# Three PSUM banks that rotate between the two products of a scan step, and one 128-row product for dt's factor, B and C

## The reference, cut to what matters

```python
xs = silu(conv3(x_c));  x_dbl = xs @ W_x.T           # W_x: (64 + 16 + 16) x 256
dt_param, Bp, Cp = x_dbl[..., :64], x_dbl[..., 64:80], x_dbl[..., 80:]
dt = softplus(dt_param @ W_dt.T + b_dt) + 1e-05
A_disc = exp(-exp(A_log) * dt[..., None])             # one factor for each of 16 states
Bx = Bp[:, :, None, :] * dt[..., None] * xs[..., None]
s = A_t * s + Bx_t;  ssum = s.sum(-1)                 # a scan over the tokens for each state
y = (Cp @ W_C.T) * ssum + D_param * xs
```

## Time and profile before

| | |
|---|---|
| three runs | 1262.65, 1260.84, 1262.3 us; median 1262.3 |
| profiled execution | 1258.12 us; its span 1256.3 us |
| busy share of the span | TensorE 83%, VectorE 56%, GpSimd 54%, ScalarE 50% |
| mean granted clock of TensorE | 0.901 of full |

### The profile page before, as it was taken

How to read it: one execution, slowest core, us unless ns; L and a number is a source line. 1 busy time by engine, 2 the same in 40 slices (tenths; PEclk the granted TensorE clock), 3 DMA queues, 4 the chain that set the end, 5 groups by cost and what they waited for, 6 DMA issues and landing times. The chain is left out here.

```text
span 1256.3 us, 15452 instructions
## 1 busy us (share of the span) xinstructions
PE 1043.6 (83%) x4736; PEld 832.8 (66%) x4736; DVE 705.6 (56%) x1280; ACT 625.3 (50%) x1190; POOL 681.0 (54%) x605
## 2 busy tenths in 40 slices
PE   4555578887867887797988899969999999999995
PEld 2122265664644655575777688859999999999884
DVE  1699998999988899976796442101111111111045
ACT  3784869778476586668554432212232222232234
POOL 2495967759469786578665347324343433332221
PEclk9676778898887897898999899979999999999998
DMA  5000010202002007113322589359998888887252
GB/s 180 18 28 6 34 34 18 68 1 83 2 1 84 1 18 227 42 22 110 83 96 67 172 236 208 55 150 347 337 316 266 264 276 251 262 273 227 41 176 101
DMA packets 140931, 162.68 MB, mean 129 GB/s; under 512 B 27976, under 2 KB 125984, under 8 KB 140832
## 3 DMA queue, kind: packets, MB, share of 16 engines
q1 hardware_dynamic: 124976, 142.70, 36.0%
q0 software_dynamic: 15872, 18.99, 7.7%
HBM read 135.20 MB, written 26.87 MB: 129 GB/s over the span
## 5 line engine op out<-in xcount | busy, mean ns | idle before, releaser
L1542 POOL TENSOR_TENSOR Ssum<-Ssum,S 128x512 f32<-128x512 f32 x240 | 301.5, 1270 | 105.9 <-DVE S L1162 104.7
L1014 PE MATMUL psum<-w,hT 128*128 128x256 f32 x1152 | 260.0, 384 | 4.2 <-issue 4.2
L1014 PEld LDWEIGHTS psum<-w,hT 128*128 128x128 f32 x1152 | 219.8, 193 | 34.4 <-issue 4.6
L1592 POOL DMA_INDIRECT acc_d<-y,ID x72 | 114.3, 1587 | 236.8 <-DMA acc_d<-y,ID 124.7
L1431 ACT ACTIVATE A<-dts,nea 128x512 f32<-128x512 f32 x256 | 177.3, 720 | 68.6 <-DVE S L1162 40.4
L1470 ACT ACTIVATE hT<-psum,bb 128x256 f32<-128x256 f32 x200 | 83.5, 470 | 244.7 <-PE psum L981 244.7
L981 PE MATMUL psum<-XT,w 128*128 128x256 f32 x800 | 182.8, 386 | 7.4 <-issue 6.5
L1138 DVE TENSOR_TENSOR psum<-us,psum 128x512 f32<-128x512 f32 x256 | 163.4, 682 | 31.6 <-PE psum L902 29.6
L981 PEld LDWEIGHTS psum<-XT,w 128*128 128x128 f32 x800 | 154.0, 194 | 33.9 <-issue 10.7
L1162 DVE TENSOR_TENSOR_SCAN S<-A,carry,psum 128x512 f32<-128x512 f32 x120 | 148.8, 1264 | 0.0
L1296 DVE TENSOR_TENSOR y<-bb,psum 128x256 f32<-128x256 f32 x72 | 27.0, 416 | 209.0 <-PE psum L1014 209.0
(11 more groups left out here) (149 smaller groups left out, 1314.3 us busy)
## 6 DMA issues: line engine op xcount, KB each, us to landing
w<-W SPq DMA_DIRECT2D x94, 1024.0 KB, 6.7
bb<-b SPq DMA_DIRECT2D x47, 128.0 KB, 7.8
xnb<-x SPq DMA_DIRECT2D x16, 256.0 KB, 3.0
Xr<-x SPq DMA_DIRECT2D x16, 256.0 KB, 4.6
x_d<-gb SPq DMA_DIRECT2D x8, 512.0 KB, 2.9
xn_d<-nb SPq DMA_DIRECT2D x8, 512.0 KB, 3.3
X<-x_d SPq DMA_DIRECT2D x16, 256.0 KB, 9.3
ACC<-acc_d SPq DMA_DIRECT2D x16, 256.0 KB, 5.9
```

What stands on the lines that cost most here:

```text
L1014: t = eng.matmul(bank(g)[:, 256 * k:256 * k + 256], hT[n % 2][:, f, 128 * k:128 * k + 128], w[:, f, :], start=f == 0, stop=f == 7)
L1542: eng.tensor_tensor(to, to, of, ALU.add).then_inc(nsum, 1)
L1592: eng.indirect_dma_start(acc_d, bass.IndirectOffsetOnAxis(ap=ID[:, col, 1:2].bitcast(u32), axis=0), y[n % NY][:, k, :], None, compute_op=A ...
```

## The change

1. The three banks rotate. `spread` of step m writes bank m mod 3. The first product of `mult` writes bank (m - 1) mod 3, which the step before has used, the second goes in place as before. `spread` then waits for one scan less, `mult` for one scan more.
2. `dtc` and `bp` become one product `dbc` of 128 rows: four times 16 rows of B (in the fourth, of C) and 16 rows of dt's factor. It is copied once to f32 (`dbc`) and once to bf16 (`bst`). `dt` then multiplies 128 rows, with zeros in `wdt` where B and C stand; `cmat` reads rows 96 to 111. `dbc_out` stands in PLAN where `bp_out` stood.
3. At the start the zeroing of `wx` on GpSimd and the wait for it go; `wx` is loaded by 8 DMAs in place of 5, and `wdt` is 128 x 256 in place of 64 x 256.
4. The five other banks rotate over one use less in each chunk, so that some products take a bank that another one has left.

```diff
-        BB, UB = PS[0:2], PS[2]
+        BB = PS[0:3]
...
-                        eng.wait_ge(scan, 2 * (m - 1))
-                    eng.matmul(BB[m % 2], SEL[:, n:n + 1].to_broadcast([96, 128]), bst[i % 2],
+                        eng.wait_ge(scan, 2 * m - 3)
+                    eng.matmul(BB[m % 3], SEL[:, n:n + 1].to_broadcast([96, 128]), bst[i % 2],
...
-                    bb = BB[m % 2]
+                    bb, ub = BB[m % 3], BB[(m - 1) % 3]
...
-                            eng.wait_ge(scan, 2 * m - 1)
-                        eng.tensor_tensor(bb if c else UB, us[i % 2][:, c, :], bb, ALU.mult).then_inc(mult, 1)
+                            eng.wait_ge(scan, 2 * m)
+                        eng.tensor_tensor(bb if c else ub, us[i % 2][:, c, :], bb, ALU.mult).then_inc(mult, 1)
...
-                    eng.tensor_tensor_scan(to, A[m % NA], BB[(m // 2) % 2] if c else UB, first,
+                    eng.tensor_tensor_scan(to, A[m % NA], BB[(m // 2 - 1 + c) % 3], first,
...
-                        t = eng.matmul(ps[0:80, :], wx[:, k, 0:80], xs[i % 2][:, k, :], start=k == 0, stop=k == 1)
-                    t.then_inc(full[BANK[g]], 1)
-                elif step == "bp":
-                    i, g = a
-                    ps = take(g)
-                    for k in range(2):
-                        t = eng.matmul(ps[0:96, :], wx[:, k, 80:176], xs[i % 2][:, k, :], start=k == 0, stop=k == 1)
+                        t = eng.matmul(ps, wx[:, k, :], xs[i % 2][:, k, :], start=k == 0, stop=k == 1)
...
-                    eng.matmul(ps, wdc[0:64, 128 * c:128 * c + 128], dcb[i % 2][0:64, :],
+                    eng.matmul(ps, wdt[:, 128 * c:128 * c + 128], dbc[i % 2],
...
-                    eng.matmul(ps, wdc[64:80, 128 * c:128 * c + 128], dcb[i % 2][64:80, :],
+                    eng.matmul(ps, wc[:, 128 * c:128 * c + 128], dbc[i % 2][96:112, :],
...
-                    eng.copy(dcb[i % 2], ps[0:80, :]).then_inc(dtc_out, 1)
-                elif step == "bp_out":
-                    i, g = a
-                    ps = evacuate(g)
+                    eng.copy(dbc[i % 2], ps).then_inc(dbc_out, 1)
                     if i >= 2:
                         eng.wait_ge(mult, 32 * (i - 1))
-                    eng.copy(bp32, ps[0:96, :]).then_inc(bp_out, 1)
                     eng.copy(bst[i % 2], ps[0:96, :]).then_inc(bp_out, 1)
...
-                    eng.wait_ge(bp_out, 2 * i + 2)
-                    eng.tensor_tensor(bp32[0:64, :], bp32[0:64, :], bst[i % 2][0:64, :], ALU.subtract).then_inc(mid, 1)
+                    eng.wait_ge(bp_out, i + 1)
+                    eng.wait_ge(xT_out, 2 * i + 2)
+                    eng.tensor_tensor(bp32, dbc[i % 2][0:64, :], bst[i % 2][0:64, :], ALU.subtract).then_inc(mid, 1)
...
-            eng.wait_ge(wx_zero, 1)
-            for to, fr, n in [(0, 0, 64), (64, 80, 16)] + [(80 + 32 * g, 64, 16) for g in range(3)]:
-                eng.dma_start(wx[:, :, to:to + n], wxv[:, :, fr:fr + n]).then_inc(got_wx, 16)
-            eng.dma_start(wdc[0:64, :], W_dtT).then_inc(got_v, 16)
-            eng.dma_start(wdc[64:80, :], W_CT).then_inc(got_v, 16)
+
+            for k in range(4):
+                eng.dma_start(wx[:, :, 32 * k:32 * k + 16], wxv[:, :, (80 if k == 3 else 64):][:, :, 0:16]).then_inc(got_wx, 16)
+                eng.dma_start(wx[:, :, 32 * k + 16:32 * k + 32], wxv[:, :, 16 * k:16 * k + 16]).then_inc(got_wx, 16)
+            eng.dma_start(wdt, W_dtT).then_inc(got_v, 16)
+            eng.dma_start(wc, W_CT).then_inc(got_v, 16)
```

More of the change, by code:

```diff
@@ L142, in prep @@
         yield
-        d, p, t0, t1 = (next(use) for _ in range(4))
-        say("dtc", i, d)
+        d, t0, t1 = (next(use) for _ in range(3))
+        say("dbc", i, d)
         yield
-        say("bp", i, p)
-        say("dtc_out", i, d)
         yield
-        say("bp_out", i, p)
+        say("dbc_out", i, d)
         yield
@@ L523, in finishing @@
     say("result", NC - 1)
-TAKING = {"xT", "nT", "xc", "z", "dtc", "bp", "dt", "cmat", "wout", "logit", "count", "turn", "up", "down"}
-GIVING = {"xT_out", "nT_out", "xc_out", "z_out", "dtc_out", "bp_out", "dt_sum", "yadd", "gated", "lg_out",
+TAKING = {"xT", "nT", "xc", "z", "dbc", "dt", "cmat", "wout", "logit", "count", "turn", "up", "down"}
+GIVING = {"xT_out", "nT_out", "xc_out", "z_out", "dbc_out", "dt_sum", "yadd", "gated", "lg_out",
           "place", "turn_out", "up_out", "down_out"}
@@ L547, in emptied @@
         return "xc_out", 6 * i + 3 * n + 3
[L548 to L551, removed]
+    if step == "dbc":
+        return "bp_out", i + 1
     if step == "dt":
@@ L726, in build @@
         zs = [put(f"zs{i}", [128, 4, 256]) for i in range(2)]
-        dcb = [put(f"dcb{i}", [80, 512]) for i in range(2)]
+        dbc = [put(f"dbc{i}", [128, 512]) for i in range(2)]
         bst = [put(f"bst{i}", [96, 512], bf16) for i in range(2)]
+        wc = nc.alloc_sbuf_tensor_at("wc", [128, 256], f32, offset=at[0] - 1024).ap()[96:112, :]
         A = [put(f"A{i}", [128, 512]) for i in range(NA)]
@@ L767, in build @@
         xc_out, conv, edged, xs_done, zs_done = (sem(n) for n in ("xc_out", "conv", "edged", "xs_done", "zs_done"))
-        dtc_out, bp_out, mid, mid_out, low, low_out = (
-            sem(n) for n in ("dtc_out", "bp_out", "less_high", "mid_out", "less_mid", "low_out"))
+        dbc_out, bp_out, mid, mid_out, low, low_out = (
+            sem(n) for n in ("dbc_out", "bp_out", "less_high", "mid_out", "less_mid", "low_out"))
         dt_out, softp, dt_done = sem("dt_out"), sem("softplus"), sem("dt_done")
@@ L868, in _ @@
                     t.then_inc(full[BANK[g]], 1)
-                elif step == "dtc":
+                elif step == "dbc":
                     i, g = a
@@ L1384, in _ @@
                     exp_ln()
-                elif step == "dtc_out":
+                elif step == "dbc_out":
                     i, g = a
@@ L1400, in _ @@
                     eng.wait_ge(mid, i + 1)
[L1401 removed]
+                    eng.copy(bst[i % 2][0:64, :], bp32).then_inc(mid_out, 1)
                 elif step == "low_out":
@@ L1481, in _ @@
         def _(eng):
-            eng.memset(wx, 0.0).then_inc(wx_zero, 1)
             eng.wait_ge(got_c, 48)
```

19 lines of the change are left out of this document (10 added, 9 removed).

## The result

| | before | after |
|---|---|---|
| median of 14 runs each, us | 1263.91 (1260.84 to 1270.02) | 1273.45 (1268.94 to 1275.98) |
| ratio, 95% interval | | 1.0072, 1.0059 to 1.0084 |
| profiled execution, us | 1258.12 | 1275.98 |
| end of the last scan in it | 692.8 | 706.3 |
| mean granted clock of TensorE | 0.901 | 0.888 |

The kernel is slower by 0.72%, where the forecast was no change, and its time lies beyond the range (1257.8 to 1268.5).

What follows compares the result with a forecast made beforehand. VectorE was taken to bound the stretch of the scans, TensorE what follows. Terms 5.2 + 0 - 1.9 - 0.2 - 2.3 + 0, plus 0.2 for the clock, gave +1.0 us: 1263.3 in the median, range 1257.8 to 1268.5.

Steps and rivals of the forecast that it cites:

- Part 1: VectorE's first product of each step waits for the scan just before it: 45 paid waits at 0.115 us, +5.2 us.
- parts 3 and 4: One product less saves VectorE 1.9 us in chunk 2, 0.2 in chunk 0; a free dt bank 2.3 in chunk 5.
- How often it is paid: Of 88 first products directly behind a scan on VectorE, 45 were forecast to pay the wait, the rest hidden by other waits.
- Part 2: TensorE may write a bank for spread one scan earlier: value 0, ends -4.0 and +2 us if its clock recovers later.
- Part 5: At the start, three more load issues cost ScalarE 1.5 us, an earlier dt gains 1.5: sum 0, -0.7 to +0.7.
- TensorE's clock, +0.2: An added allowance of 0.2 us for TensorE's clock, bringing the sum from +0.8 to +1.0 us.
- Rival B: Slower: the wait at each step's first product (L1138) paid nearly everywhere, 8.3 us less 4.4 gains, 1266.2; chance 0.32.

Runs made afterwards that it cites:

- the swapped waits (2): The changed kernel with the two waits of each step's first product written in the other order, the scan's first; ratio to before 1.0073.
- the waiting scans (3): The kernel before, with each step's first scan waiting for its step's second product, the instruction just ahead; ratio 1.0055.
- the wait alone (1): The kernel before, with only the first product of each step waiting for the scan just ahead; ratio 1.0058.
- (6): The changed kernel with spread waiting for both scans of step m - 2 again, as before; ratio 1.0041, and with the product's waits also swapped 1.0038.
- (4): The kernel before with only the merged product added, its eight loads of wx issued after wg; ratio 0.9965, against 1.0004 with the loads in place.

## Why the prediction was wrong

Two terms of the sum failed. The forecast was +1.0 us and the medians moved by 9.5. Part 1 stood at +5.2 and measured 7.8 by itself (1.0058); parts 3 and 4 stood at -4.4 together and measured nothing (1.0004, 0.9989 to 1.0020, with their loads). The second miss is the larger one.

- **Part 1, the price of the wait, mis-sized.** It was 0.115 us each, with 0.15 as the upper end. It is 0.18, and 0.21 with the longer products. The row it was taken from, the stats behind their product, waits with one semaphore, and that price is right: the swapped waits (2) and the waiting scans (3) show the same 0.03 to 0.04 us. But the product waits for two things, and the wait for the scan sits in the semaphore instruction ahead, which adds 0.07. The prediction read the neighbours of the wait, not its form. By the rule of the Trainium skill that it named ("VectorE: DVE Perf Modes", section "The DRAIN you can't avoid"), the term would be 0; the wait alone (1) and the waiting scans (3) decide against it for these instructions.
- **How often it is paid.** The guess was 45 of 88, or 51%. Gross 18.5 us left 7.8, a share of 42%: right in kind. Where was not right. The full price is paid in chunk 0, and in chunks 2 to 5 next to nothing is left of it.
- **Part 2, the earlier bank, 0 with an end of +2 for the clock.** No gain came, as said, and the reason was the right one. The slow stretch did move onto products that VectorE waits for, as the end said; in after itself that accounts for 0.4 of the 2.9 us that the waits at steps 101 to 103 grew by (6).
- **Parts 3 and 4 (-1.9, -0.2 and -2.3): the waits went, the time did not.** This step of the prediction took a wait that vanishes for time that is gained. The waits at steps 42, 43 and 92 went, and with the merged product alone step 10's 0.1 us too. But each gain was eaten by a VectorE instruction close by that GpSimd's chain held: in chunk 2 the small operation took 3.4 to 3.6 us more, and in chunk 5 the comparison of the logits took 2.3 us more with the merged product alone and 1.9 in after. In chunk 5 the gain could not last, since that instruction is held until GpSimd's chain ends, and the chain did not end earlier. In chunk 2 it is no consequence of the edit: the wait alone, which has no merged product, hit the additions too (3.69 us). The trace of before had both in plain sight, the small operation with 4.78 us at 468.65 and the comparison with 2.25 us at 492.75, ten times the 0.22 of its like. And the waits for `spread` fell to 29.2 us in all, not to 25, since those of steps 101 to 103 grew.
- **Part 5, the start, 0.** ScalarE's first work came at 14.48 (forecast 14.6), `dts` at 37.83 for 37.59: right. What it missed is that the order of the loads was worth about 5 us (4).
- **TensorE's clock, +0.2.** No row gave this term. With the merged product alone the mean granted clock of all runs is 0.890, against 0.900 of before beside it; up to 400 us TensorE is busy for 242 us, not 250, at 0.78, not 0.81. This may give back some of each saved product; how much was not told apart.
- **Rival B** named the price of the wait and the place. But it had the wait paid nearly everywhere and the gains of 4.4 us coming in, and neither was so. Less than half was paid, at a higher price, and no gain came. That "slower" came out is no proof of its account.

## What to carry to other kernels

A buffer scheme that makes an engine wait for its own last instruction, to free another engine earlier, cost that engine 0.12 to 0.18 us here wherever the two instructions stood side by side, even if the one ahead is done "anyway": read from a trace what such a pair takes, and with as many semaphores as the new code will have. Before moving anything on a queue that is the bound, look for its instructions whose durations vary from 0.14 to 4.8 us at one shape, or from 0.22 to 6.8: they wait for something that is not shown as a wait, and they swallow or fake the effect of other edits. A stall that vanishes is a gain only if nothing behind it waits until a fixed moment; follow the saved time, step by step, to the end of the stretch. And an earlier start for work that was not late moves a pause, it doesn't remove one; ask what will run behind the pause.

## What the runs showed that was not expected

- Of two waits of one instruction, the one written last went into a separate semaphore instruction. Written first it cost VectorE 0.12 us, written last 0.18.
- A VectorE instruction on 128 x 4 elements with both inputs in SBUF took 0.13 us where GpSimd paused and up to 4.8 us in the middle of its additions, through three or four of them. One on 128 x 64 elements, also with both inputs in SBUF, took 0.22 us or up to 6.84, held through six of GpSimd's instructions. A third (`scale<-mv,C`, 128 x 4) took 0.23 us or up to 2.6, in every kernel here.
- Profiles differ in the first scan by some 2 us (46.43 and 48.41 in two kernels whose start is the same), and behind the last scan by up to 5, with the chip. So the length of a single execution of this kernel is no measure of a few us. Between these, before's two profiles agree to 0.2 us at each step that the table in 1 has, so that the steps of two kernels can be compared.
